# An attention kernel on one core: the first quad's exponentials move beside its maxima, and three of four half batches leave through DRAM

## The reference

```python
xn = _layernorm(x, axis=-1)
Q = _rope(split_heads(xn @ wq.T), THETA)      # (2, 16, 1024, 8)
K = _rope(split_heads(xn @ wk.T), THETA)
V = split_heads(xn @ wv.T)
scores = jnp.einsum('bhqd,bhkd->bhqk', Q, K) * scale
scores = jnp.where(causal_mask, -jnp.inf, scores)
attn = jax.nn.softmax(scores, axis=-1)
out = jnp.einsum('bhqk,bhkd->bhqd', attn, V).transpose(0, 2, 1, 3).reshape(B, N, D) @ wo.T
ffn = jnp.einsum('bsk,nk->bsn', xn, CB) * (SCB * (1.0 / 127.0)) + bias
return x + out + ffn
```

## Time and profile before

| | us |
|---|---|
| median of 3 runs | 279.49 |
| lowest, highest | 278.91, 283.0 |
| profiled execution | 278.35 |
| its span in the trace | 276.6 |
| PE, DVE, ACT, POOL busy | 242.5, 211.2, 187.0, 105.4 |

### The profile page before, as it was taken

The page is one execution under the profiler, slowest core; times in us unless marked ns, Lnnn a source line. Parts: engine busy times, 40 slices in busy tenths (PEclk is TensorE's granted clock), DMA queues, the critical chain, the costliest instruction groups (busy, mean ns, idle before and its releaser), DMA issues.

```text
span 276.6 us, 11045 instructions
## 1 busy us (share of the span) xinstructions
PE 242.5 (88%) x4736; PEld 125.3 (45%) x4736; DVE 211.2 (76%) x601; ACT 187.0 (68%) x366; POOL 105.4 (38%) x171
## 2 busy tenths in 40 slices
PE   0695788745989999999999999999999999999894
PEld 0342644103433544544455445445655444567552
DVE  5899277872899999989997899999998988414203
ACT  0425433403986789778779878986788898898741
POOL 7644992494703440492087014304301330430020
PEclk9999999955999999999999999999999999999999
DMA  7515857580004161016007001500800000000102
GB/s 202 187 28 142 213 125 140 120 207 4 4 1 117 41 154 28 4 46 133 7 4 164 14 4 46 134 2 15 162 9 4 4 5 4 5 23 25 43 21 59
DMA packets 21017, 18.29 MB, mean 66 GB/s; under 512 B 2516, under 2 KB 20308, under 8 KB 20968
## 3 DMA queue, kind: packets, MB, share of 16 engines
q1 hardware_dynamic: 20392, 17.00, 25.1%
q10 hardware_dynamic: 576, 0.59, 0.8%
HBM read 12.12 MB, written 5.24 MB: 63 GB/s over the span
## 4 chain that ended last, share of the span: by engine, by line
PE 63%; DVE 12%; POOL 8%; ACT 5%; DMA 5%; issue 3%; SPq 3%; ACTq 0%; POOLq 0%
PE psV L910 20%; PE psB L841 19%; PE psA L841 17%; DVE prod L743 7%; PE psA L945 4%; ACT ring L646 3%; DVE xn L701 2%; DMA k_scratch<-ot 2%; POOL x_sb L508 2%; POOL xnT L447 2%; POOL ot L440 2%; SPq L342 2%; PE psB L824 2%; DMA x_sb<-x 2%; SPq L356 1%
## 5 line engine op out<-in xcount | busy, mean ns | idle before, releaser
L743 DVE CUSTOM_DVE_ANT_0 prod<-psA,cmask 128x128 f32<-128x128 f32 (+7 forms) x256 | 179.2, 754 | 30.4 <-PE psA L841 28.3
L646 ACT ACTIVATE ring<-psB 128x512 f32<-128x512 f32 x288 | 154.7, 602 | 33.3 <-PE psB L841 29.8
L841 PE MATMUL psB<-qs,ks 128*32 128x512 bf16 (+3 forms) x1536 | 101.3, 329 | 1.8 <-ACT ring L646 0.9
L841 PE MATMUL psA<-ks,qs 128*32 128x512 bf16 (+3 forms) x1536 | 94.7, 334 | 6.3 <-DVE mx L743 3.7
L910 PE MATMUL psV<-ring,va 128*32 128x512 f32 (+3 forms) x768 | 75.9, 486 | 0.4 <-POOL ring L492 0.3
L492 POOL TENSOR_SCALAR_AFFINE_SELECT ring<-ring 128x512 f32<-128x512 f32 x64 | 39.5, 635 | 74.4 <-ACT ring L646 74.2
L841 PEld LDWEIGHTS psB<-qs,ks 128*32 128x32 bf16 x1536 | 41.0, 97 | 46.3 <-ACT ring L646 21.8
L841 PEld LDWEIGHTS psA<-ks,qs 128*32 128x32 bf16 x1536 | 34.7, 97 | 44.2 <-DVE mx L743 24.7
L910 PEld LDWEIGHTS psV<-ring,va 128*32 128x32 f32 x768 | 22.5, 110 | 16.0 <-issue 8.7
L472 POOL CAST shifts<-mx 128x16 bf16<-128x16 f32 x16 | 3.1, 196 | 63.5 <-DVE mx L743 63.5
L761 DVE RECIPROCAL rden<-psA 128x32 f32<-128x32 f32 x8 | 2.8, 354 | 24.3 <-PE psA L945 24.3
(11 more groups left out here) (80 smaller groups left out, 163.7 us busy)
## 6 DMA issues: line engine op xcount, KB each, us to landing
qs<-q_scratch SPq DMA_DIRECT2D x48, 96.0 KB
ks<-k_scratch SPq DMA_DIRECT2D x48, 96.0 KB
q_scratch<-ot SPq DMA_DIRECT2D x20, 128.0 KB, 2.5
k_scratch<-ot SPq DMA_DIRECT2D x12, 128.0 KB, 2.5
x_sb<-x SPq DMA_DIRECT2D x4, 256.0 KB, 4.8
rope_sb<-rope SPq DMA_DIRECT2D x2, 512.0 KB, 6.2
y<-xn SPq DMA_DIRECT2D x8, 128.0 KB, 1.8
w_sb<-weights ACTq DMA_DIRECT2D x1, 256.0 KB, 3.4
```

The lines of the kernel that those rows point to most:

```text
L646: act.activation(ring[:, s % P_RING, k * HALF:(k + 1) * HALF], bank_b(e % B_RING), ACT.Exp)\
L743: last = dve.tensor_tensor_reduce(masked_scores[:, u % 2, at:at + w], psA[:, (u % 2) * SEQ + at:(u % 2) * SEQ + at + w], cmask[:, SEQ - w: ...
L841: mm = pe.matmul(psum[strip:strip + STRIP, at:at + size], keys[:, strip:strip + STRIP], queries, start=True, stop=True)
```

## The change

Two things change, and the tables around them.

**The start of quad 0.** Of its 22 units 17 stay ahead; the last five stand beside banks 0 (one), 3 (three) and 4 (one). Its second turn of maxima is no task any more, but stands beside bank 5. POOL follows the same count of banks (`beside` with `SPLIT_BANK`, `LATE_SPLIT`): first the split of half 0, then the rotations of tasks 4 and 5, then the split of half 1; the rotations of tasks 6 and 7 come at banks 19 and 22. The tasks on PE stand closer together, all before unit 8. The copies of parts 4 and 5 on ACT go to banks 5 to 14. The numbers of the other quads' rows in the tables are new as well.

**The output.** For three half batches (both of batch 0, the first of batch 1) each saved quad is stored by DMA in `o_scratch` in DRAM. Two DMAs load them back with the 128 channels on the partitions (`heads_t`) and with each head's sum repeated 8 times beside them (`dens`). DVE takes the reciprocal of 128x512 and multiplies 128x512, PE multiplies by wo directly (`project_half`), DVE adds 128x512. The last half of batch 1 goes the old way, in two groups. The turns of its first three quads stand behind the last values now.

```diff
@@ -33,76 +33,84 @@
...
+ORDER = [(0, 1) for i in range(QUADS)]
+HALF_STEPS = [[(D0, 0, 0), (D1, 0, None), (D2, 0, None)],
+              [(FULL, 1, kb) for kb in range(4)] + [(D0, 1, 4), (D1, 1, None), (D2, 1, None)]]
+STEPS = [[step for hf in ORDER[i] for step in HALF_STEPS[hf]] for i in range(QUADS)]
...
-    [AHEAD, AHEAD, AHEAD, AHEAD, AHEAD, AHEAD, AHEAD, AHEAD, AHEAD, AHEAD, AHEAD, AHEAD, AHEAD, AHEAD, AHEAD, AHEAD, AHEAD, AHEAD, AHEAD, AHEAD, AHEAD, AHEAD],
...
+    [AHEAD, AHEAD, AHEAD, AHEAD, AHEAD, AHEAD, AHEAD, AHEAD, AHEAD, AHEAD, AHEAD, AHEAD, AHEAD, AHEAD, AHEAD, AHEAD, AHEAD, 36, 39, 39, 39, 40],
+    [4, 5, 6, 7, 9, 9, 12, 14, 14, 15, 15, 18, 19, 19, 20, 22, 23, 24, 26, 27, 27, 30],
...
+    [AHEAD, 41],
...
+    [13, 14, 22, 26, 28, 33, 34, 35, 39, 41],
...
+    [15, 18, 20, 25, 29, 32, 34, 35, 35, 35],
...
+    [22, 53],
...
-SPLIT_MASKS = [[0, 0], [4, 8], [12, 12], [19, 20], [28, 29], [36, 36], [43, 44], [51, 52]]
+SPLIT_BANK = [[-3, -1], [-26, 3], [-31, -5], [-26, -15], [-22, -17], [-22, -19], [-11, -7], [-31, -10]]
+LATE_SPLIT = [[-2, 8, 14], [-2, 10, 17], [19, 30, 38], [22, 30, 40]]
+LATE_BANK = [[5, 12], [8, 14], [22, 32], [26, 34]]
...
-EARLY = {250: 0, 258: 1, 267: 2, 268: 3, 272: 4, 279: 5}
-TURN_BACK, PROJECT = 4, 6
+HALVES = [(0, 0), (0, 1), (1, ORDER[QUADS - 1][0])]
+LAST_HALF = ORDER[QUADS - 1][1]
+PROJECT_BANK = [264, 274, 293]
+TURN_FIRST = 293
+GROUPS = 2
...
-TASKS = [("late", 4), ("late", 5), ("v", 0), ("v", 1), ("ffn", 0), ("ffn", 1), ("late", 6), ("max", 0), ("late", 7),
-         ("max", 1)]
+TASKS = [("late", 4), ("late", 5), ("v", 0), ("v", 1), ("ffn", 0), ("ffn", 1), ("late", 6), ("late", 7),
+         ("max", 0)]
...
-TASK_AFTER = {0: (3, 0), 1: (3, 1), 3: (4, 0), 4: (4, 1), 5: (5, 0), 6: (5, 1), 8: (6, 0), 9: (6, 1), 11: (7, 0), 12: (8, 0),
-              13: (8, 1)}
+TASK_AFTER = {(3, 0): 0, (3, 1): 0, (4, 0): 1, (4, 1): 1, (5, 0): 2, (5, 1): 3, (6, 0): 4, (6, 1): 4, (7, 0): 5, (7, 1): 5, (8, 0): 7}
...
+        heads_t = rot
+        dens = rest
...
+        o_scratch = nc.dram_tensor("o_scratch", [len(HALVES), QUAD * QUAD, STRIP, HALF], F32)
...
+        def half_bank(h):
+
+            return bank_a((0, 1, 3)[h])
...
+            def store_heads(i, hf):
+
+                h = HALVES.index((i // 4, hf))
+                sp.wait_ge(ot_saved, 2 * i + ORDER[i].index(hf) + 1)
+                rows = o_scratch[h, (i % 4) * QUAD:(i % 4 + 1) * QUAD, :, :].rearrange("j r t -> (j r) t")
+                sp.dma_start(rows, ot[:, i, hf * HALF:(hf + 1) * HALF]).then_inc(o_stored[h], 16)
+
+            def load_heads(h):
+
+                sp.wait_ge(o_stored[h], 16 * QUAD)
+                if h == 2:
+                    sp.wait_ge(half_filled, 1)
+                sp.dma_start(heads_t[:, h % 2, :], o_scratch[h, :, 0:DH, :]).then_inc(o_loaded[h], 16)
+                sp.dma_start(dens[:, h % 2, :], o_scratch[h, :, DH:DH + 1, :].to_broadcast([QUAD * QUAD, DH, HALF]))\
+                    .then_inc(o_loaded[h], 16)
...
-            store_parts(2)
             store_shifts(0, 1)
             for i in range(1, QUADS):
-                store_shifts(i, 0)
+                store_shifts(i, ORDER[i][0])
+                if i == 1:
+                    store_parts(2)
+                store_shifts(i, ORDER[i][1])
                 if i == 1:
                     store_parts(3)
-                store_shifts(i, 1)
+                for done, hf in ((i - 2, 1), (i - 1, 0)):
+                    if done >= 0 and (done // 4, hf) in HALVES:
+                        store_heads(done, hf)
...
+                if i == 5:
+                    load_heads(0)
+                if i == 6:
+                    load_heads(1)
+            store_heads(QUADS - 1, 0)
+            load_heads(2)
...
+            def beside(n):
+                for i in range(QUADS):
+                    for hf in ORDER[i]:
+                        if NBANKS * i + SPLIT_BANK[i][hf] == n:
                             split_maxima(i, hf)
-
-            def steps(i, which):
-                done = i * NMASKS + MASK_END[which[0]] - MASKS[which[0]]
-                for s in which:
-                    for m in range(MASKS[s]):
-                        mask(i, s, m)
-                        done += 1
-                        splits(done)
-
+                for c in range(LATE, 2 * LATE):
+                    if LATE_SPLIT[c - LATE][0] == n:
+                        rotate_all(c)
+                for c in range(LATE, 2 * LATE):
+                    if LATE_SPLIT[c - LATE][1] == n:
+                        leave(c)
+                for c in range(LATE, 2 * LATE):
+                    if LATE_SPLIT[c - LATE][2] == n:
+                        third_part(c)
...
+            for n in (-3, -2, -1):
+                beside(n)
...
-            for n in range(len(TASKS) - 1):
+            for n in range(len(TASKS)):
                 save_task(n)
-            for n in range(2):
-                parts_of(4, n)
-                parts_of(5, n)
-            save_task(len(TASKS) - 1)
...
+            def normalise_half(h):
+                dve.wait_ge(o_loaded[h], 2 * 16)
+                dve.reciprocal(dens[:, h % 2, :], dens[:, h % 2, :]).then_inc(dens_ready, 1)
+                dve.wait_ge(dens_ready, h + 1)
+                dve.tensor_tensor(heads_t[:, h % 2, :], heads_t[:, h % 2, :], dens[:, h % 2, :],
+                                  ALU.mult).then_inc(heads_ready, 1)
...
+            def half_result(h):
+                b, hf = HALVES[h]
+                tiles = slice(TPB * b + 4 * hf, TPB * b + 4 * hf + 4)
+                dve.wait_ge(half_filled, h + 1)
+                dve.tensor_tensor(y_sb[:, tiles, :].rearrange("p t d -> p (t d)"), half_bank(h),
+                                  x_sb[:, tiles, :].rearrange("p t d -> p (t d)"), ALU.add).then_inc(half_ready, 1)
...
+            dve.wait_ge(part3, 8)
+            normalise_half(0)
+            normalise_half(1)
             dve.wait_ge(xb_ready, 8)
-            for g in range(GROUPS):
-                normalise_heads(g)
-                if g > 0:
-                    result(g - 1)
-            result(GROUPS - 1)
+            half_result(0)
+            half_result(1)
+            normalise_half(2)
+            half_result(2)
+            normalise_heads(0)
+            normalise_heads(1)
+            result(0)
+            result(1)
...
+            def project_half(h):
+                pe.wait_ge(a_drained, QUADS * NUNITS)
+                pe.wait_ge(heads_ready, h + 1)
+                for m in range(4):
+                    mm = turn_tile(half_bank(h)[:, m * P:(m + 1) * P], heads_t[:, h % 2, m * P:(m + 1) * P], w_sb[:, 5, :])
+                mm.then_inc(half_filled, 1)
+
             def early(n):
-                if n - PROJECT in EARLY:
-                    project(EARLY[n - PROJECT])
-                if n - TURN_BACK in EARLY:
-                    turn_back(EARLY[n - TURN_BACK])
-                for m in range(2):
-                    if n - m in EARLY:
-                        turn(EARLY[n - m], m)
+                for h in range(len(HALVES)):
+                    if PROJECT_BANK[h] == n:
+                        project_half(h)
+                if TURN_FIRST == n:
+                    for g in range(GROUPS):
+                        for m in range(2):
+                            turn(g, m, range(3))
```

More of the change, by code:

```diff
@@ L296, in attention_ffn_kernel @@
         ot_saved = sem("ot_saved")
+        o_stored = [sem(f"o_stored{h}") for h in range(3)]
+        o_loaded = [sem(f"o_loaded{h}") for h in range(3)]
+        dens_ready = sem("dens_ready")
+        heads_ready = sem("heads_ready")
+        half_filled = sem("half_filled")
         o_turned = sem("o_turned")
@@ L311, in turned @@
         def turned(eng, i, hf):
-            if i == 0:
+            if i == 0 and hf == 0:
                 eng.wait_ge(task_saved, TASKS.index(("max", hf)) + 1)
@@ L552, in _ @@
                 copy_v(i, 0)
-                steps(i, (0,))
-                if i == 0:
-                    leave(6)
-                steps(i, (1,))
-                if i == 0:
-                    leave(7)
-                wait(pool, pv_done, i * NSTEPS)
-                copy_v(i, 1)
-                steps(i, (2,))
-                if i == 1:
-                    for n in range(4):
-                        add_ffn(n)
-                if i == 2:
-                    for n in range(4):
-                        add_bias(n)
-                steps(i, (7,))
-                if i == 0:
-                    third_part(6)
-                    third_part(7)
-                steps(i, (8, 9))
+                for n in range(NBANKS):
+                    beside(i * NBANKS + n)
+                    if ORDER[i][0] == 1 and n == FULL_BANKS:
+                        wait(pool, pv_done, i * NSTEPS)
+                        copy_v(i, 1)
+                    for s in range(NSTEPS):
+                        if BANK_END[i][s] - 1 == n:
```

(18 more changed lines are left out.)

205 lines of the change are left out of this document (100 added, 105 removed), and 27 rows, old and new, of tables (UNIT_BANK, VALUE_BANK).

## The result

The changed kernel takes 269.92 us (median of 5 runs, 269.56 to 271.12); the kernel before, run on the same chip, 279.77 us (5 runs). The ratio is 0.966, with a 95% interval of 0.963 to 0.969: 3.4% faster. 269.2 us had been forecast.

What follows compares the result with a forecast made beforehand. PE was taken as the bound. Last values at 255.7, the third half batch's chain to DVE's reciprocal at 259.9, plus 6.4 of tail gave span 266.3; plus 1.75 around it 268.1, plus 1.1 for the median 269.2 us; range 264.5 to 275.5.

Steps and rivals of the forecast that it cites:

- the two mechanisms: DVE going from quad 0 to quad 1 without the gap, 5.6 us; less PE work behind bank 249, 6.8 us.
- The start: Quad 1 on DVE starts at 61.2 instead of 66.85 us, no longer waiting for split and rotations: gain 5.6 us.
- The delay of unit 6 by 4.0 us: In quad 0, five half tasks now ahead of unit 6 cost 5.3 us, less 1.3 us of filled PE idle time.
- most of which goes: DVE's 3.4 us of idle time from 41 to 60.2 us mostly vanishes, leaving quad 1 0.8 us later.
- the rival of the earlier clock: PE half idle from about 48 us, clock falls, some 2 to 3 us lost; time 272; chance 0.24 with worse order.
- The worse order: New tables lose some 2 to 3 us in quads 1 to 7; time 272; chance 0.24 shared with earlier clock.
- the rival that would have made the kernel slower: Values placed too soon before need cost each quad 1.8 us, 12.6 us in all; time 281 to 286; chance 0.07.
- the sum of PE's steps and the old waits: Bank 249 to last values: banks 8.6, values 11.5, projections 1.8, with the same waits 25.0 us.
- The step that fewer matmuls: Bank 249 to last values: fewer turns, turns back and projections on PE, 6.8 us less.
- The chain of the third half batch: After quad 7's first half is saved: store 3.0, loads 3.9, reciprocal 3.9, multiply 0.7 us; expected to end last.
- no wait for the half batch: Rival: PE goes from the last values at 255.7 to the projection at once; time 265.9; chance 0.20.
- the projection of 0.88 us on PE; the turns of three quads of four, 0.84 us: PE's work behind the third half batch's multiply, in the tail, before the last quad's turns of 0.3 to 0.4 us.

Runs made afterwards that it cites:

- short_tail: Changed kernel with the half saved four banks sooner, all last-half turns ahead of the third projection, and DVE serving the last groups first; 265.92 us, ratio 0.950.
- early_save: Changed kernel with the values of quad 7's first half beside banks 15 to 17 and its save four banks sooner; 268.08 us, ratio 0.955.
- start_only: Changed kernel with its start and tables, but output in eight groups the old way, six beside the last banks; 274.15 us, ratio 0.978.
- no_third_reciprocal: Changed kernel without DVE's reciprocal for the third half batch, which is left unnormalised; 266.72 us, ratio 0.952.
- turns_first: Changed kernel with the turns of the last half's first three quads ahead of the third half batch's projection on PE; 267.50 us, ratio 0.955.
- split_first: Kernel before, with POOL's split of quad 0's second maxima moved ahead of the rotations of tasks 6 and 7; 278.26 us, ratio 0.994.
- tasks_spread: Changed kernel with the halves of the late rounds behind units 0 to 13 instead of 0 to 7; 268.29 us, ratio 0.956.
- short_tail_spread: short_tail with quad 7's first values and save where the changed kernel has them, plus tasks spread over units 0 to 13; 264.96 us, ratio 0.945.

## Why the prediction was right, and where it was off

The sign, the size and the two mechanisms held. By its own steps, each stretch as forecast and as the profiled run has it:

| stretch | forecast | measured |
|---|---|---|
| start of quad 1 | 61.2 | 62.5 |
| from there to bank 249 | 169.5 | 169.8 |
| bank 249 to the last values | 25.0 | 24.0 |
| last values to the reciprocal of the last groups | 4.2 | 7.0 |
| rest of the tail | 6.4 | 6.1 |
| span | 266.3 | 269.4 |

(Bank 249 is the fourth exponential of a row of six that starts at 230.88 and takes 3.04 us: 230.88 + 3 x (3.04 - 0.6) / 5 = 232.3.)

- **The start** was forecast to gain 5.6 us and gained 4.3 in the profiled run. The delay of unit 6 by 4.0 us was exact. Mis-sized was the step "most of which goes", on DVE's idle time: behind the clock of 0.50 DVE waits once for 0.78 us and four times for about 0.1. That was the rival of the earlier clock, in small. Other kernels with the same start have quad 1 at 61.3 (short_tail) to 62.7 (early_save), so part of it is the run; and start_only gained 5.6 us in its median, with times 3.7 us apart.
- **Quads 1 to 7** took 0.3 us more than forecast. The worse order, and the rival that would have made the kernel slower, did not come: PE idles for 2.5 us in 171.5.
- **Bank 249 to the last values** was 1.0 us quicker than the sum of PE's steps and the old waits; the wait ahead of the last save is 1.63 us in place of 2.20. The step that fewer matmuls (1.8 us of projections in place of turns, turns back and projections for six groups) are worth 6.8 us on PE held.
- **The chain of the third half batch** was forecast at 11.5 us from the end of the save to the end of the multiply, and took 10.9 (247.56 to 258.44): store and loads 6.8 (6.9), reciprocal 3.35 (3.9), multiply 0.7. The Trainium skill (VectorE: DVE Perf Modes, "First, the fixed hardware budget") gives the reciprocal a repeat count of 8, from which 4.3 us were estimated; the trace has 3.35 us, or 6.5 ns an element, and the measurement decides. Its save came 1.3 us later, with bank 249. So PE's wait was 2.35 us, for 2.1 forecast. The rival "no wait for the half batch" was wrong, as no_third_reciprocal shows by taking the wait away.
- **The term that was mis-sized** is "the projection of 0.88 us on PE; the turns of three quads of four, 0.84 us" and the last quad's 0.3 to 0.4: 2.1 us forecast, 4.67 measured from 258.59 to 263.26. The projection took 1.41 us until the first turn at the clock of 0.60 (0.87 in turns_first at the full clock), 85 turns 1.59 us at 0.50 (96 in 1.06 in turns_first), together 1.2 us for the clock; then comes the stop of 1.17; and 43 turns 0.49. The forecast priced matmuls from a stretch in which PE never idled, and put them behind a wait of 2 us.
- **Luck.** The sum for the profiled execution was 268.1 and that was 271.1, 3.0 us more. To the sum 1.1 us was added, by which the median of before stood above its profiled run; after, the profiled run stands 1.2 above the median. This hid 2.3 us of the error: against the median 269.9 the sum without it is 1.8 short.

Left open: what sets the time of PE's stop within the turns (last section), which of the start's last two parts closes the gap, and why split_first, tasks_spread and early_save have times in two places 2 to 3 us apart; only one run of each was profiled.

## What to carry to other kernels

When work that is off the path is batched up into few large steps (a load, a reciprocal of 512 elements, a projection), look for what stands behind it in the queue of the bounding engine: here one number, which put 96 short matmuls ahead of the wait instead of behind it, was worth 2.9 us, and all of them ahead, with the projection and that half batch's add behind, 6.4. Price work that follows a wait at both levels of the clock and not only at that of the busy stretch: behind some 2 us of idle time both were seen here. And an edit named for its effect is to be tested in its parts: moving the split alone gave 1.6 us of 5.6, and the exponentials beside the first quad's maxima, for which the change is named, nothing clear of the noise. And where a gain seen early in a trace does not reach the end, follow it to the place where it is lost: in short_tail_spread that was a stop in the tail.
